# Attention with maxima found first: four projection buffers, two requesters for the first rows of k, and a float32 product beside each early maximum

## What is computed

```python
q = (x @ Wq.T + bq).reshape(B, T, H, D)
k = (x @ Wk.T + bk).reshape(B, T, H, D)
v = (x @ Wv.T + bv).reshape(B, T, H, D)
scores = jnp.einsum('bqhd,bkhd->bhqk', q, k) * attn_scale[0]
scores = jnp.where(mask[None, None], -jnp.inf, scores)
attn = jax.nn.softmax(scores, axis=-1)
out = jnp.einsum('bhqk,bkhd->bqhd', attn, v).reshape(B, T, C)
```

## Time and profile before

| | before |
|---|---|
| median of 3 runs | 457.44 us (456.29 to 462.58) |
| the profiled execution | 459.99 us, span 458.0 us |
| PE busy | 424.8 us (93%) |
| DVE busy | 345.8 us (76%) |
| ACT busy | 224.2 us (49%) |
| POOL busy | 144.6 us (32%) |

### The profile page before, as it was taken

How to read it: one execution, slowest core, us unless ns; L and a number is a source line. 1 busy time by engine, 2 the same in 40 slices (tenths; PEclk the granted TensorE clock), 3 DMA queues, 4 the chain that set the end, 5 groups by cost and what they waited for, 6 DMA issues and landing times.

```text
span 458.0 us, 7639 instructions
## 1 busy us (share of the span) xinstructions
PE 424.8 (93%) x2430; PEld 198.3 (43%) x2430; DVE 345.8 (76%) x977; ACT 224.2 (49%) x301; POOL 144.6 (32%) x251
## 2 busy tenths in 40 slices
PE   5979999999999999999999998999999999999992
PEld 2622222223223232322235434676776666666660
DVE  2849789778897989799975573867598689856864
ACT  3530056446676868677776886232532342323220
POOL 5065235724837654443644433000000000000000
PEclk9985569559999999999999999999999999999998
DMA  4554205520210202000000004333233324433330
GB/s 126 167 209 131 69 4 155 165 83 14 59 36 13 72 3 64 10 2 1 4 2 3 3 2 96 101 108 104 70 99 111 105 71 133 144 122 94 115 97 23
DMA packets 27383, 34.21 MB, mean 75 GB/s; under 512 B 6096, under 2 KB 16464, under 8 KB 27344
## 3 DMA queue, kind: packets, MB, share of 16 engines
q1 hardware_dynamic: 26240, 33.01, 24.1%
q10 hardware_dynamic: 1104, 0.73, 0.6%
HBM read 29.07 MB, written 4.46 MB: 73 GB/s over the span
## 4 chain that ended last, share of the span: by engine, by line
PE 71%; DVE 16%; issue 6%; DMA 3%; ACT 2%; ACTq 1%; POOL 1%; DVEq 0%; POOLq 0%
PE ps L1393 14%; PE ps L1439 12%; PE ps L1309 12%; DVE comb_rows L1033 7%; PE ps L1408 7%; PE ps L1410 7%; PE ps L1409 7%; PE ps L1376 5%; DVE mx L1036 3%; PE ps L1312 2%; PE ps L1323 2%; DMA bk<-in_bk 1%; ACT probs L927 1%; DVE x L1101 1%; DVE mx L1033 1%
## 5 line engine op out<-in xcount | busy, mean ns | idle before, releaser
L927 ACT ACTIVATE probs<-ps 128x1024 f32<-128x1024 f32 (+2 forms) x160 | 144.9, 940 | 65.1 <-PE ps L1376 63.9
L1033 DVE CUSTOM_DVE_ANT_0 comb_rows<-ps,score_mask 128x512 f32<-128x512 f32 (+1 forms) x192 | 117.5, 664 | 20.8 <-PE ps L1309 19.8
L1309 PE MATMUL ps<-rows_k,rows_q 48*128 48x512 bf16 (+3 forms) x384 | 114.0, 372 | 13.5 <-DVE mx L1033 7.7
L966 ACT ACTIVATE rows_q<-ps 128x512 f32<-128x512 f32 x68 | 40.6, 598 | 97.4 <-PE ps L1410 94.8
L1393 PE MATMUL ps<-probs,Vg 128*32 128x512 f32 (+3 forms) x768 | 85.8, 521 | 1.6 <-ACT probs L927 1.1
L1036 DVE TENSOR_REDUCE mx<-ps 128x2 f32<-128x512 f32 (+3 forms) x128 | 70.2, 586 | 13.4 <-PE ps L1312 9.4
L1309 PEld LDWEIGHTS ps<-rows_k,rows_q 48*128 48x128 bf16 x384 | 30.9, 96 | 112.0 <-DVE mx L1033 68.8
L1376 PE MATMUL ps<-rows_q,rows_k 51*128 51x512 bf16 (+3 forms) x384 | 74.6, 345 | 2.0 <-ACT probs L927 1.9
L1408 PE MATMUL ps<-x1hi,w_hi 128*128 128x512 f32 x136 | 74.0, 544 | 0.0
L1247 DVE TENSOR_TENSOR rows_q<-ps,rows_q 128x512 f32<-128x512 f32 x64 | 44.1, 689 | 36.2 <-PE ps L1439 34.9
L1439 PE MATMUL ps<-rows_k,w_down 128*128 128x512 f32 x136 | 69.5, 593 | 0.7 <-DVE rows_k L1252 0.7
(11 more groups left out here) (117 smaller groups left out, 352.4 us busy)
## 6 DMA issues: line engine op xcount, KB each, us to landing
comb_rows<-weights SPq DMA_DIRECT2D x128, 128.0 KB, 2.9
scratch<-oT SPq DMA_DIRECT2D x8, 384.0 KB, 2.7
w_raw<-in_unitT SPq DMA_DIRECT2D x17, 128.0 KB, 2.7
rows_q<-scratch SPq DMA_DIRECT2D x16, 96.0 KB
rows_k<-scratch SPq DMA_DIRECT2D x14, 96.0 KB
w_down<-in_unitT SPq DMA_DIRECT2D x1, 1088.0 KB, 6.9
xT<-in_xT SPq DMA_DIRECT2D x4, 256.0 KB, 6.0
rows_q<-scratch SPq DMA_DIRECT2D x16, 64.0 KB
```

The costliest lines, as they stand in the source:

```text
L927: act.activation(dst, src, ACT.Exp).then_inc(exps_ready, 1)
L1033: dve.tensor_tensor_reduce(masked_scores[k % 4][:, 0:m], src[:, 0, :], score_mask[:, 0:m], 1.0, LAST, ALU.add, ALU.max, to).then_inc(max_r ...
L1309: mm = pe.matmul(dst[:, at * m:(at + 1) * m], rows_q[f:f + ROWS, s, p + qt * P:p + (qt + 1) * P], rows_k[f:f + ROWS, s, p + k0:p + k0 + m] ...
```

## The change

- `q32` and `r32` get four buffers each, in the space of `probs`, so a copy waits for the split of piece n - 4. ScalarE waits for GpSimd's two splits in front of the later steps.
- For group 0, ScalarE asks for the first half of the rows of k (three DMAs) and GpSimd for the second half (three DMAs). ScalarE copies the last two projections before the last three quarters of V.
- GpSimd clears `Vg` before it waits for the mask.
- `HOLD` is 5 instead of 10, and behind each of the steps ahead of the first exponential TensorE runs one more product of `wq` with 192 columns of `xT` that nobody reads.

```diff
-HOLD = 10
+HOLD, BESIDE = 5, 192
...
+BY_DVE, BY_POOL = (0, 1, 2, 3, 4, 5), (6, 7)
...
-        q32 = oT[:, 0, :].rearrange("p (s n) -> p s n", s=2)
-        r32 = oT[:, 1, :].rearrange("p (s n) -> p s n", s=2)
+        q32, r32 = probs[:, 0, :, :], probs[:, 1, :, :]
...
+        def wait_rows(eng, g):
+            eng.wait_ge(rows_loaded[g % NS], 192 * (g // NS + 1) - (48 if g % NS == 0 else 0))
+            if g == 0:
+                eng.wait_ge(first_k_loaded, 48)
...
-        def load_k(eng, g):
+        def load_k(eng, g, halves=(0, 1), signal=None):
...
-            for f in range(2):
+            for f in halves:
...
             pool.memset(half[:, :], -0.5).then_inc(consts_set, 1)
+            pool.memset(Vg[:, :, :, :, :], 0.0).then_inc(consts_set, 1)
+            pool.wait_ge(consts_set, 2)
+            pool.memset(Vg[:, :, :, :, D:D + 1], 1.0).then_inc(consts_set, 1)
+            pool.wait_ge(consts_set, 3)
             pool.memset(score_mask[:, :], 0.0).then_inc(mask_set, 1)
...
+            pool.wait_ge(ones_set, NS)
+            pool.wait_ge(k_stored[0], 32)
+            load_k(pool, 0, (1,), first_k_loaded)
             for n in (6, 7):
                 split_rest(n)
...
             def copy_projection(n):
                 act.wait_ge(proj_done, n + 1)
-                if n >= 2:
-                    act.wait_ge(parts_ready, n - 1)
+                if n - 4 in BY_DVE:
+                    act.wait_ge(parts_ready, BY_DVE.index(n - 4) + 1)
+                elif n - 4 in BY_POOL:
+                    act.wait_ge(rest_ready, BY_POOL.index(n - 4) + 1)
...
             copy_values(0)
-            copy_values(1)
             copy_projection(5)
             act.wait_ge(ones_set, NS)
             act.wait_ge(k_stored[0], 32)
-            load_k(act, 0)
+            load_k(act, 0, (0,))
+            copy_projection(6)
+            copy_projection(7)
+            copy_values(1)
             copy_values(2)
             copy_values(3)
-            copy_projection(6)
-            copy_projection(7)
+
+            act.wait_ge(rest_ready, len(BY_POOL))
...
+            first_exps = next(k for k, step in enumerate(pe_order) if step[0] == "e")
+            for kind, _, n in pe_order[:first_exps]:
+                max_step(*MSEQ[n])
+                pe.matmul(bank(VALUES, BESIDE), wq[:, :], xT[:, 0:BESIDE], start=True, stop=True)
             used = 1
-            for kind, g, n in pe_order:
+            for kind, g, n in pe_order[first_exps:]:
```

More of the change, by code:

```diff
@@ L494, in build @@
         max_set = sem("max_set")
+        first_k_loaded = sem("first_k_loaded")
         mask_set = sem("mask_set")
@@ L645, in load_k @@
                     eng.dma_start(rows_k[ROW_HALF * f + at:ROW_HALF * f + at + n, s, :],
-                                  src).then_inc(rows_loaded[s], 16)
+                                  src).then_inc(signal or rows_loaded[s], 16)
         pe_order, act_order, pool_order, _ = attention_order()
@@ L680, in load_rows, with wait_parts @@
                     load_k(sp, g)
+            def wait_parts(n):
+                if n in BY_DVE:
+                    sp.wait_ge(parts_ready, BY_DVE.index(n) + 1)
+                else:
+                    sp.wait_ge(rest_ready, BY_POOL.index(n) + 1)
             for n in range(NC):
-                sp.wait_ge(parts_ready, n + 1)
+                wait_parts(n)
                 store_parts(n)
@@ L687, in _ @@
             load_rows(1)
[L688 to L692, removed]
+            for n in range(NC, 2 * NC):
+                wait_parts(n)
                 store_parts(n)
@@ L771, in _ @@
             pool.tensor_copy(score_mask[:, 0:P], mask_qk[:, :]).then_inc(mask_set, 1)
[L773 to L776, removed]
             def values(g):
@@ L822, in split_rest @@
             def split_rest(n):
-                s, k = n % 2, 2 * (n - 6)
+                s, k = n % 4, 2 * BY_POOL.index(n)
                 pool.wait_ge(proj_copied, 2 * n + 2)
@@ L889, in copy_projection @@
                 act.wait_ge(proj_done, n + 1)
-                if n >= 2:
-                    act.wait_ge(parts_ready, n - 1)
+                if n - 4 in BY_DVE:
+                    act.wait_ge(parts_ready, BY_DVE.index(n - 4) + 1)
+                elif n - 4 in BY_POOL:
+                    act.wait_ge(rest_ready, BY_POOL.index(n - 4) + 1)
                 how = dict(scale=scale[:, 0:1], bias=bqs[:, 0:1]) if n % 2 == 0 else dict(bias=bk[:, 0:1])
-                act.activation(q32[:, n % 2, :], bank(PROJ[n]), ACT.Identity, **how).then_inc(proj_copied, 1)
+                act.activation(q32[:, n % 4, :], bank(PROJ[n]), ACT.Identity, **how).then_inc(proj_copied, 1)
                 act.activation(parts[:, n, 0, :], bank(PROJ[n]), ACT.Identity, **how).then_inc(proj_copied, 1)
@@ L1004, in _ @@
             dve.memset(mx[:, :, :, :], LAST).then_inc(max_set, 1)
-            for n in range(6):
-                s = n % 2
+            for k, n in enumerate(BY_DVE):
+                s = n % 4
                 dve.wait_ge(proj_copied, 2 * n + 2)
                 dve.tensor_tensor(r32[:, s, :], q32[:, s, :], parts[:, n, 0, :], ALU.subtract).then_inc(split_steps, 1)
-                dve.wait_ge(split_steps, 2 * n + 1)
+                dve.wait_ge(split_steps, 2 * k + 1)
                 dve.tensor_copy(parts[:, n, 1, :], r32[:, s, :]).then_inc(split_steps, 1)
-                dve.wait_ge(split_steps, 2 * n + 2)
+                dve.wait_ge(split_steps, 2 * k + 2)
                 dve.tensor_tensor(parts[:, n, 2, :], r32[:, s, :], parts[:, n, 1, :],
@@ L1289, in max_step @@
                 if kind == "unit" and n == 0:
-                    pe.wait_ge(rows_loaded[g % NS], 192 * (g // NS + 1))
+                    wait_rows(pe, g)
                 if r < RING:
@@ L1365, in exp_unit @@
                 if n == 0:
-                    pe.wait_ge(rows_loaded[s], 192 * (g // NS + 1))
+                    wait_rows(pe, g)
                 if n == 0 or BLOCKS[EXPU[n - 1][0]][0] != qh:
```

## The result

| | before | after |
|---|---|---|
| median of 4 runs each | 460.01 us (456.29 to 462.86) | 507.67 us (503.69 to 510.6) |
| ratio | | **1.104**, 95% interval 1.0958 to 1.1121 |
| the profiled execution | span 458.0 us | span 503.1 us, 504.86 us |
| first exponential's scores start | 58.30 us | 101.69 us |

The change makes the kernel a tenth slower. The forecast was 464.6 us, with 451 to 484 as its range; the time lies outside, on the side of the rival "the clock falls before the maxima and stays low", which the range left out.

The account below looks back on a forecast made before the run. The wait for the rows of k, then 52 steps at VectorE's pace, bound the kernel; products would make TensorE the bound. First exponential +8.8, behind it -1.6, together +7.2 us on 457.44: 464.6 us, range 451 to 484.

Parts of the forecast that it names:

- the clock falls before the maxima and stays low: Rival: TensorE at 1.2 GHz through the 52 steps, first exponential 36.5 us late, 494 us; chance 0.2.
- the leading products held 1.00, and the new ones are of the same kind: Argument that products beside the maxima keep TensorE at full clock, as those ahead of the scores did.
- what decides is where the clock stands just behind the first scores: Sign for a low clock during the maxima; if it comes back on the way, 470 to 484 us.
- the prediction's own gap: TensorE idle ahead of the first scores, from 23.0 to 25.1 us: 2.1 us against 0.71 before.
- The rival's price: Low clock over the 52 steps: own work about 24, products 34.2, changes 11.5, together 69.7 us; time 494 us.
- The rows of k: Start of attention: earlier cast, four buffers and split requests land them at 25.1 instead of 28.0, gaining 2.9 us.
- The changes between 48 and 128 rows: TensorE's switches between scores and products cost 0.10 and 0.14 us each, 11.5 us over the 52 steps.
- The 0.14: Fixed time in us from a 128-row product to the next 48-row score, charged behind all 52 steps.
- The rival with free changes: Switches between scores and products cost nothing, products fit under VectorE's pace: -4.3 us, 453.1 us; chance 0.17.
- Behind the first exponential: From first to fifth exponential, ScalarE's waits for TensorE shrink at full clock: 1.6 us come back.
- The sum: Whole kernel: +8.8 us to the first exponential, -1.6 us after it, +7.2 us in all, 464.6 us.

Follow-up runs that it names:

- nine leading products: Changed kernel with nine instead of five products ahead of the first scores: 473.16 us, ratio 1.0234.
- dense stretch: Changed kernel with four more products of 512 columns behind the ninth step: 485.05 us, ratio 1.0394.
- seven leading products: Changed kernel with seven instead of five products ahead of the first scores: 508.34 us, ratio 1.1009.
- five, later: Changed kernel whose five products ahead of the scores wait for the first copy of the seventh projection: 478.37 us, ratio 1.0217.
- two of three: Changed kernel with nine products ahead of the scores and one behind only two of every three steps: 462.52 us, ratio 0.9894.
- every second: Changed kernel with nine products ahead of the scores and one behind only every second step: 469.53 us, ratio 1.003.
- before, with the products: Kernel before plus only the 52 products of 192 columns: three runs 467.06 to 471.57 us, the fourth 514.75; ratio 1.0152.
- 96 columns: Changed kernel with nine products ahead of the scores and 96 instead of 192 columns behind each step: 493.2 us, ratio 1.0579.
- before, two of three: Kernel before, ten products ahead of the scores, plus products behind two of three unmasked units only: 482.33 us, ratio 1.0251.
- no products: Changed kernel without the 52 products beside the maxima: 463.2 us, ratio 0.9953.
- the two kernels without products: Changed kernel without the 52 products, GpSimd's requests kept (463.2 us, ratio 0.9953) or all six on ScalarE (462.93 us, ratio 0.9968).

## Why the prediction was wrong

**The failed step** is the argument against the low clock, "the leading products held 1.00, and the new ones are of the same kind", by which it got 0.2. The products do hold the clock, but only one that is full when they begin (nine leading products). They do not bring a low one back: from 30 to 101.69 us they run without a pause at 0.50, and four products of 512 columns without scores between them restore it (the dense stretch; the five leading products do it when they are started later). What decides is whether the clock survives the gap in front of the first scores, and it does not survive the prediction's own gap either: 2.1 us assumed, 1.77 enough with seven leading products. The prediction saw the place ("what decides is where the clock stands just behind the first scores") and had a gap with a fall 3 us behind it in its rows; it gave the weight to the wrong side.

The gaps in front of the first score and what the clock did behind it up to the first exponential, each in one profiled execution:

| kernel | gap us | product behind | clock |
|---|---|---|---|
| five, later | none | each step | 1.00 |
| two of three | none | two of three | 1.00 |
| every second | none | every second | falls within 34 to 36 us |
| nine leading | 0.07 | each step | 1.00 |
| before, with the products | 0.42 | each step | 1.00 |
| 96 columns | 0.91 | each step, half as wide | falls within 28 to 30 |
| before, two of three | 1.18 | two of three | falls within 30 to 32 |
| seven leading | 1.77 | each step | falls within 26 to 27 |
| changed kernel | 3.25 | each step | falls within 28 to 30 |
| dense stretch | 3.54 | each step | falls within 26 to 28 |

Between 0.42 and 1.77 us only kernels with fewer or narrower products were run, so where the limit lies stays open, and with it why the kernel before with the products held its clock in three executions and was low for long in the fourth. The Trainium skill (TensorE: Matmul & The Clock Gate, "HAM oscillation — how this bites in real kernels") tells of a kernel in which each wait for a DMA lets the clock fall and the next stretch of matmuls starts slow. The gap of 3.25 us that rows_k ends in the changed kernel agrees with it in kind; that the stretch behind never recovers while TensorE has no pause is what this trace adds.

**The rival's price**, 494 us, was short too. It had the first exponential's scores at 94.8; they came at 101.69. 1.9 us of the 6.9 are the later start, 5.0 the steps: 74.7 us instead of 69.7. A unit takes 1.47 us where the rival's terms give 0.42 + 0.10 + 0.66 + 0.14 = 1.32. The product is what differs: its columns take 0.56 us and not 0.66, and the rest 0.39 and not 0.14. The rival held the rest constant at either clock; it grows with the low one, from 0.27 us.

**The rows of k.** The cast came down as forecast, 1.39 to 0.44 us. The first score was forecast at 25.1 and came at 26.97. The chain began 0.65 us later than in the execution before, and the last piece landed 5.13 instead of 3.99 us after its request, together 1.8. The Trainium skill's rule that VectorE's fast casts keep GpSimd from writing descriptors (SBUF — State Buffer, the "DVE blocks DMA" trap) does not explain the slow landing: VectorE's last cast ended at 20.01, before the third request at 21.75. It may have a part in the 0.65 us that GpSimd's first request waited (19.68 to 20.34), for that cast ran then:

```profile
19.58 0.43 DVE L1032 CAST oT<-probs 128x512 bf16<-128x512 f32 x1
```

No run here separates the two. Even so the split requests came out ahead: from the landing of the last store to that of the rows pass 7.0 to 7.3 us where GpSimd's requests end the wait (changed kernel, no products, seven leading) and 8.05 to 8.95 with six on ScalarE (four kernels), where the forecast had 6.1. What the start was worth is shown by the two kernels without products: nothing measurable in the time, with either requester.

**The changes between 48 and 128 rows.** With the clock at full, 52 steps took 44.0 us where the forecast said 42.0, and 0.83 us a unit for 0.78. This term was right in kind and nearly in size. The split was not: the columns of a product are 0.26 us and not 0.33, the rest 0.27 and not 0.14. The 0.14 was read from value products, which load weights of 128x32, while the new product loads 128x128 twice; whether that is the difference was not tested. The rival with free changes is refuted by the same rows. The Trainium skill's rule of the weight load that is pulled ahead (TensorE: Matmul & The Clock Gate, "Step-by-step: what each phase is for"), which the prediction put beside that rival, did not make the products free for this pair of shapes; that the weight load is what costs the 0.27 us is not shown.

**Behind the first exponential.** 1.6 us were to come back. With a full clock 5.99 - 4.17 = 1.8 did (nine leading products); in the changed kernel none, since the clock was still low there.

**The sum, had the clock held:** 473.16 us, ratio 1.0234. The forecast's 464.6 was within reach of it (7.2 us forecast over before, 2.34% or some 11 measured); 2.0 us of the difference are the steps and 1.45 the later start, 26.55 instead of 25.1. The gap's cost on top is 1.104 against 1.0234, some 37 us of 460: 44.0 to 74.7 us for the steps and 4.2 to 6.3 for the first exponentials are 33 of them.

## What to carry to other kernels

A filler product has two prices, one at each clock, and it keeps a clock better than it wins one back: look first at the last pause in front of it, then at the filler. Close that pause, or put a dense stretch behind it; 4.6 us of matmuls gave back over 21 us here. A low clock that another engine's pace covered cost nothing measurable here, so price a filler against that engine's pace, and give it only to the steps where TensorE has time to spare under it.

## What the runs showed of the hardware

- The same sequence of scores and products ran at 1.00 for all of its 44 us in one kernel and at 0.50 for over 70 us in the other, with no pause of TensorE in either; the difference was a gap of 3.25 us, or of 1.77, against one of 0.07 in front of it.
- A float32 product of 128 rows between scores of 48 rows takes 0.27 us at 2.4 GHz and 0.39 at 1.2 beside its columns (two widths, 96 and 192).
- Masked pairs of scores and identity products did not hold a full clock that the units ahead of them had held (0.89 in 40 to 46 us, 0.50 behind, in one execution).
- Three pieces of rows_k on GpSimd beside three on ScalarE landed in 6.5 us from GpSimd's first request to the last landing (20.34 to 26.88), against 8.0 for six on ScalarE before (20.02 to 27.99). 0.65 us of waiting stood ahead of GpSimd's first request, and the kernel's time does not show the rest.
